# Block attention, heavy half: the value projection moved from the even to the odd step of each pair, the turn of the routed rows put ahead of it

## What is computed

```python
def heavy_attn(xq, context, scores_kv, gamma, wq, wkv_t, wo):
    ...
    q = (xqn @ wq).reshape(b, nq, HEADS, DH).transpose(0, 2, 1, 3) * SCALE
    ...
    kv = jnp.einsum('rhdi,brni->brhnd', kvw, ctx)
    k, v = jnp.split(kv, 2, axis=-1)
    ...
    attn = jax.nn.softmax(jnp.einsum('bhid,bhjd->bhij', q, k), axis=-1)
    out = jnp.einsum('bhij,bhjd->bhid', attn, v)
    out = out.transpose(0, 2, 1, 3).reshape(b, nq, HID)
    return out @ wo
...
light_out = light_local_attn(x, gamma_light, wq_light, wkv_light, wo_light)
...
heavy_out = jnp.zeros_like(x).at[jnp.arange(b)[:, None], idx_q].set(routed_out)
return light_out + heavy_out
```

## Time and profile before

| | |
|---|---|
| time, median of 3 runs (lowest to highest) | 2456.97 us (2455.01 to 2460.59) |
| the profiled execution, its own time | 2473.0 us |
| its span, first to last instruction | 2470.1 us |
| PE busy over the span | 93% |
| the chain that ended last, PE's share | 81% |
| the heavy half in the trace | about 556 to 955 us |

### The profile page before, as it was taken

The page is one execution under the profiler, slowest core; times in us unless marked ns, Lnnn a source line. Parts: engine busy times, 40 slices in busy tenths (PEclk is TensorE's granted clock), DMA queues, the critical chain, the costliest instruction groups (busy, mean ns, idle before and its releaser), DMA issues.

```text
span 2470.1 us, 42459 instructions
## 1 busy us (share of the span) xinstructions
PE 2287.0 (93%) x16226; PEld 1667.0 (67%) x16226; DVE 1332.3 (54%) x2963; ACT 978.0 (40%) x2336; POOL 628.1 (25%) x555
## 2 busy tenths in 40 slices
PE   6987999999999998898999999988984999999998
PEld 3554677776666665554676655544653999999997
DVE  7776654764444546765556533358665444444442
ACT  1576555454444543443233321235652222222222
POOL 3444222261010003202123100034454222222222
PEclk8999999999999999998999999989996999999999
DMA  6124101130010000120001049300238222222221
GB/s 213 59 94 134 35 18 69 35 120 18 27 52 27 26 27 26 63 74 28 1 1 37 0 148 331 132 0 21 84 134 344 33 36 36 36 36 36 36 36 27
DMA packets 85408, 165.95 MB, mean 67 GB/s; under 512 B 12984, under 2 KB 66105, under 8 KB 82753
## 3 DMA queue, kind: packets, MB, share of 16 engines
q1 hardware_dynamic: 48064, 114.05, 13.7%
q0 software_dynamic: 16368, 26.23, 5.4%
q10 hardware_dynamic: 20784, 23.06, 3.0%
HBM read 118.46 MB, written 77.51 MB: 79 GB/s over the span
## 4 chain that ended last, share of the span: by engine, by line
PE 81%; DVE 8%; ACT 5%; issue 2%; POOL 2%; DMA 1%; another core or an unknown queue 0%; SPq 0%; DVEq 0%; ACTq 0%; POOLq 0%
PE PS L2474 14%; PE PS L2500 7%; PE PS L2930 5%; PE PS L1649 5%; PE PS L2942 4%; PE PS L1640 4%; PE PS L2159 3%; PE PS L2171 3%; PE PS L674 3%; PE PS L2999 3%; PE PS L2990 3%; DVE mem L1223 3%; PE PS L756 3%; PE PS L2964 3%; PE PS L3035 2%
## 5 line engine op out<-in xcount | busy, mean ns | idle before, releaser
L2474 PEld LDWEIGHTS PS<-ctx2T,x_all 128*128 128x128 f32 x3124 | 361.7, 193 | 10.1 <-DVE x_all L2623 6.6
L2474 PE MATMUL PS<-ctx2T,x_all 128*128 128x128 f32 x3124 | 362.3, 276 | 5.9 <-DVE x_all L2623 5.1
L2671 POOL DMA_INDIRECT out_x<-xnT,moe_small x71 | 127.9, 1801 | 431.3 <-ACT xnT L2556 428.5
L2500 PE MATMUL PS<-mem,moe_small 128*128 x852 | 195.7, 379 | 0.8 <-ACT xnT L2556 0.8
L2623 DVE COPY x_all<-mem 128x2816 f32 x71 | 115.5, 1627 | 106.7 <-issue 93.7
L2500 PEld LDWEIGHTS PS<-mem,moe_small 128*128 128x128 f32 x852 | 156.3, 190 | 19.5 <-issue 1.2
L1223 DVE TENSOR_REDUCE mem<-PS 128x32 f32<-128x2048 f32 x48 | 109.9, 2290 | 76.2 <-PE PS L699 75.5
L3461 POOL TENSOR_TENSOR mem<-mem,moe_small 128x512 f32<-128x512 f32 x64 | 82.2, 1303 | 208.3 <-DVE moe_small L3326 208.3
L3316 DVE TENSOR_REDUCE moe_small<-PS 128x2 f32<-128x1024 f32 x64 | 78.4, 1226 | 98.7 <-PE PS L2990 95.9
L756 PE MATMUL PS<-mem 128*128 128x256 f32 x384 | 108.7, 436 | 20.7 <-DVE mem L1242 20.7
L3140 ACT ACTIVATE mem<-PS,moe_small 128x128 f32<-128x128 f32 x256 | 89.9, 377 | 94.0 <-DVE moe_small L3311 89.8
(11 more groups left out here) (392 smaller groups left out, 4552.8 us busy)
## 6 DMA issues: line engine op xcount, KB each, us to landing
slots<-in_trash_rows SPq DMA_DIRECT2D x8, 4290.0 KB, 63.2
mem<-in_L_ffn_experts SPq DMA_DIRECT2D x8, 2176.0 KB, 11.3
mem<-recips SPq DMA_DIRECT2D x42, 256.0 KB
xn<-slots ACTq DMA_DIRECT2D x53, 130.0 KB
x_all<-in_x SPq DMA_DIRECT2D x8, 512.0 KB, 8.4
unit_rows<-moe_small ACTq DMA_DIRECT2D x8, 512.0 KB, 3.0
xn<-unit_rows SPq DMA_DIRECT2D x8, 512.0 KB, 4.4
mem<-unit_rows SPq DMA_DIRECT2D x8, 512.0 KB
```

What stands on the lines that cost most here:

```text
L2474: last = nc.tensor.matmul(PS[:, moe_bank(j, part), c * P:(c + 1) * P], m.w[:, j % 2, k, at:at + P], m.rowT[:, j % 2, k, :], start=k == 0, ...
L2500: last = nc.tensor.matmul(PS[:, MOE_BANK_Y, 0:D], m.hT[:, j % 2, n, :], w[:, :, at:at + D], start=n == 0, stop=n == KE - 1)
L2671: nc.gpsimd.indirect_dma_start(s.T["out"], bass.IndirectOffsetOnAxis(s.token[:, j % 4:j % 4 + 1], 0), m.result[:, j % 4, :], None, compute ...
```

## The change

V is taken from the even step and put into the odd step, between T and Q, on PE; its copy goes into the odd step on ACT, between the exponentials and the copy of Q. In the last light step, V of the heavy unit 0 is put behind R, on PE and on ACT. The list of banks has R ahead of V to match, and Q of a new batch waits for the copies of the keys and of R, no more for that of V.

```diff
@@ projection_banks
-                names += [(heavy, "k", j), (heavy, "v", j)] + ([(heavy, "r", i)] if heavy and m == 0 else []) + [(heavy, "q", j)]
+                names += [(heavy, "k", j)] + ([(heavy, "r", i)] if heavy and m == 0 else []) + [(heavy, "v", j), (heavy, "q", j)]
@@ queries
         if p.heavy and m == 0:
-            pe.wait_ge(p.sems["v_ready"], j + 1)
             pe.wait_ge(p.sems["qx_ready"], i + 1)
-        else:
-            pe.wait_ge(p.sems["k_ready"], j + 1)
+        pe.wait_ge(p.sems["k_ready"], j + 1)
@@ colt_pe, light steps
-        values_of_tokens(p, nxt)
         if p.heavy:
             turn_routed(0)
+        values_of_tokens(p, nxt)
         queries(p, nxt)
@@ colt_pe, heavy steps
-        if u % QT == 0 and nxt < LIGHT_STEPS:
+        if u % QT == 1 and nxt < LIGHT_STEPS:
             values_of_tokens(heavy, nxt)
-        if u % QT == 1 and nxt < LIGHT_STEPS:
             queries(heavy, nxt)
@@ colt_act, light steps
-        copy_values(p, nxt)
         if p.heavy:
             copy_routed(0)
+        copy_values(p, nxt)
         copy_queries(p, nxt)
```

## The result

| | median us | lowest to highest | runs |
|---|---|---|---|
| before | 2456.68 | 2455.01 to 2460.59 | 4 |
| changed | 2474.21 | 2472.63 to 2474.89 | 4 |

The changed kernel takes 1.0064 of the time of before (95% interval 1.0051 to 1.0076): 17.5 us slower, where +18 was forecast.

A forecast was written before the change was run, and what follows sets the result against it. PE was taken as the bound, busy 93% of the span with 81% of the chain. Pairs +18.7 us (about 30 x 1.00 lost less 12.1 gained, plus 0.7), opening -0.7: +18, from 2457 to 2475 us, range 2464 to 2481.

The forecast's parts named there:

- Part 1: Heavy half, before the even step's S: the wait for ACT's copy of Q goes, 22 times, 12.1 us gained.
- The rival that has it stay: Before the even step's S: ACT's copy of V delays that of Q, so the old wait stays; 2487 us, 4%.
- the reading by which it stood for missing buffers: Trainium skill's reading of the repeated gap before S: a buffer shortage, so the gap stays; 2487 us.
- Part 2: Even step, before H: without V's cover H waits for DVE's copy of T, 1.00 us lost each time.
- Part 3: All heavy pairs: 22 at +0.45 us, 7 at +1.01, plus steps 0 to 3; together 18.7 us slower.
- DVE's additions: After an odd step's normalisation: additions of finished rows get more room before the next maxima and cost nothing.
- Steps 0 and 1: First heavy pair, where H already waited 1.35 us behind V: -0.4 to +1.9 us, taken as +0.7.
- Part 4: Last light step: V fills Q's 0.93 us wait for the copy of R; -0.7 us, bounds -0.9 and 0.
- The clock rival: Even steps: the new 1 us waits lower PE's clock, 1.5 us lost in each of 30, +45, 2520 us; 3%.

The follow-up runs named there:

- twice the dose: Changed kernel with DVE's copy of T put behind the normalisation in even steps 2 to 60: 2531.46 us, 1.0249 of before.
- third series: Changed kernel unaltered, measured again against the kernel before (2458.14 us) on one chip: 2472.18 us, 1.0052; with V of the first pair left in its even step, 2473.82 us.
- second series: Changed kernel unaltered, measured again against the kernel before (2471.51 us) on the slower chip: 2493.72 us, 1.009 of before.

## Why the prediction was right

The forecast of 2475 stands 0.8 us from the measured 2474.2, and the order of its terms was confirmed, but some of the terms were a little off:

- **Part 1, the old wait.** Gone, 22 times. The copy of V starts at 4.05 us after the odd S as worked out; the copy of Q at 4.84 (4.95 was estimated), so the slack is 0.43 us (0.40). The rival that has it stay, and the reading by which it stood for missing buffers, are out: the change adds none and the gap is filled.
- **Part 2, the new wait.** H starts 4.79 us after S (4.78), the loss to 3.80 is 0.99 us (1.00). Four kernels confirm the cause: with K as cover the wait is gone; less cover, V behind H, brings the wait alone; the swap of the copies moves it by 0.10 us and changes its name; a copy 0.95 us later makes the even step 0.95 us longer.
- **Part 3, the sum over pairs.** The pair is 11.57 us, not 11.65 (with R 12.02, not 12.14; with an O 13.51, not 13.58). The term that was mis-sized is V in the odd step: 1.79 us from its start to Q's, where I put the 1.88 that it takes with H behind it. 30 x 0.09 = 2.7 us: steps 2 to 61 grew by 15.4 and not by 18.0. DVE's additions cost nothing, as said.
- **Steps 0 and 1** went from 16.92 to 16.41 us, but only the first of these traces has the late copy. With it in both the difference is +4.0 (20.90), outside the upper bound of +1.9: H and O behind the wait of 3.69 us ran at the lower clock and took 1.6 us more, and the copy came 0.6 us later than in the trace of before. Without it in either it is +0.9 (16.40, and 15.50 where the first pair is kept), where I had taken +0.7. The forecast read these steps from a trace with the late copy and carried the difference over to medians that were taken, by their time, on a chip without it.
- **Part 4, the opening.** -1.0 in the first comparison (10.89 to 9.85; -0.7 forecast, bound -0.9), but +0.4 in traces where the copy of the keys is late. My bounds had no place for that.
- **The clock rival** gave 2520 and was out at this dose: granted clock 1.00 from 600 to 930 us with a wait of 0.88 us in each pair. At twice the dose it came true in part, 13.0 us.

The sum by these is 15.4 + 0.9 - 1.0 = 15.3 us where no copy is late and 15.4 + 4.0 + 0.4 = 19.8 where both are. By the medians it was 17.5 in the first comparison and 14.0 in the third series, where before took 2457 to 2458 us, and 22.2 in the second series, on the slower chip; their 95% intervals reach 3, 4 and 5 us to either side. That the forecast of 18 lies within a microsecond of the first is in part luck: by the terms it was 2.7 us too high.

## What to carry to other kernels

When a block of work is moved to fill one gap on the bound engine, ask what gap it was filling where it stood: here 1.88 us of products hid a chain of transpose, copy and answer, and their removal cost 0.99 us in each pair for 0.58 gained. Look for the second piece that can take over the cover before moving the first; with K in that place the same move was worth -0.7% and not +0.6%. A copy that comes late costs little under cover and its full length without: the one in step 0 left H a wait of 1.35 us behind V and one of 3.69 us without it.

## What the runs showed of the hardware

- The same eight products of V (128x128 in float32, 16 instructions in the trace) take 1.79, 1.88 or 1.98 us from their start to the start of what follows, with Q (128x256), H (64 columns of weights) or S (64 rows) behind them.
- Waits of PE of 0.88 us, once in each 11.6 us, never lowered its granted clock in three traces of the changed kernel; with waits of 1.8 to 2.4 us, 30 of them, it fell eight times. Behind a wait of 2.3 us in step 62 it was 13.85 us from the S of that step to the first product of the next stage in three traces and, at the lower clock, 15.4 to 15.5 in seven others; what decides between the two is open.
- One chip ran the kernel before in 2471.5 us and the others in 2457 to 2458: 11 of the 14 us between them lie in the stage between 1430 and 1910 us, which these edits do not touch.
